# Expert attention on one core: q summed on GpSimd, and three moves in the order of a step

## What is computed

```python
ss, sd = sigmoid(x @ Ws), sigmoid(x @ Wd)          # b t H E
ms, md = topk_mask(ss, 3), topk_mask(sd, 3)
ss_g, sd_g = ss * ms, sd * md
q5 = (x @ Wq).reshape(b, t, H, E, DH)
kv = (x @ Wkv).reshape(b, t, 2, H, E, DH)
k5, v5 = kv[:, :, 0], kv[:, :, 1]
q = einsum('bthed,bthe->bhtd', q5, sd_g)            # k, v alike with ss_g
attn = softmax(einsum('bhid,bhjd->bhij', q * DH ** -0.5, k))
out = einsum('bhij,bhjd->bihd', attn, v)
o5 = einsum('bthd,dm->bthm', out, Wo).reshape(b, t, H, E, 128)
y = einsum('bthem,bthe->btm', o5, md)               # and x = x + y
```

## Time and profile before

| | us |
|---|---|
| median of 3 executions | 2792.57 |
| lowest, highest | 2789.05, 2792.84 |
| the profiled execution, its own time | 2794.09 |
| its span (first to last instruction) | 2792.3 |

### The profile page before, as it was taken

How to read it: one execution, slowest core, us unless ns; L and a number is a source line. 1 busy time by engine, 2 the same in 40 slices (tenths; PEclk the granted TensorE clock), 3 DMA queues, 4 the chain that set the end, 5 groups by cost and what they waited for, 6 DMA issues and landing times. The chain is left out here.

```text
span 2792.3 us, 55544 instructions
## 1 busy us (share of the span) xinstructions
PE 2415.4 (87%) x21310; PEld 1550.2 (56%) x21310; DVE 2030.8 (73%) x3560; ACT 1517.5 (54%) x2069; POOL 1631.0 (58%) x1348
## 2 busy tenths in 40 slices
PE   6787686896999999999778999998697789999986
PEld 3555544643667667666545655555434456555554
DVE  7998455445777777776688888886386888888862
ACT  4222122322888888888435655556362255666663
POOL 1888100001999999999315677777500156777775
PEclk9999788987999999999899999999898999999998
DMA  1000000002889988999414444445401145444454
GB/s 43 1 1 1 0 23 13 1 22 65 151 152 156 162 153 154 159 159 150 111 30 79 92 92 95 95 95 99 86 1 60 28 77 95 92 92 91 92 103 78
DMA packets 763815, 226.70 MB, mean 81 GB/s; under 512 B 745992, under 2 KB 754696, under 8 KB 763552
## 3 DMA queue, kind: packets, MB, share of 16 engines
q1 hardware_dynamic: 763552, 223.16, 42.9%
HBM read 20.70 MB, written 1.05 MB: 8 GB/s over the span
## 5 line engine op out<-in xcount | busy, mean ns | idle before, releaser
L2274 PE MATMUL banks<-g_w,normed_t 128*128 128x320 f32 x1536 | 506.8, 456 | 72.4 <-DVE g_scratch L2525 69.8
L1575 POOL TENSOR_TENSOR g_p_lo<-g_p,g_p_hi 128x512 bf16<-128x512 f32 (+1 forms) x256 | 418.8, 1656 | 176.3 <-ACT g_p_hi L1559 145.8
L1764 DVE TENSOR_REDUCE at_negmax<-banks 128x1 f32<-128x1024 f32 x256 | 301.6, 1220 | 154.1 <-PE banks L1676 154.1
L2525 DVE TENSOR_TENSOR g_scratch<-banks,g_gate 128x640 f32<-128x640 f32 x384 | 314.2, 821 | 133.0 <-PE banks L2274 131.7
L2274 PEld LDWEIGHTS banks<-g_w,normed_t 128*128 128x128 f32 x1536 | 267.3, 193 | 184.5 <-DVE g_scratch L2525 111.2
L1741 POOL TENSOR_TENSOR at_p_lo<-at_p,at_p_hi 128x640 bf16<-128x640 f32 x256 | 355.4, 1402 | 13.3 <-ACT at_p_hi L1729 11.6
L1552 ACT ACTIVATE g_p<-banks,g_negmax 128x1024 f32<-128x1024 f32 x256 | 286.2, 1118 | 118.7 <-DVE g_negmax L1588 114.5
L2460 POOL TENSOR_TENSOR g_routed<-g_o,g_mask 128x640 f32<-128x640 f32 x128 | 161.1, 1259 | 303.7 <-DVE g_o L1597 303.5
L1588 DVE TENSOR_REDUCE g_negmax<-banks 128x1 f32<-128x1024 f32 x256 | 309.8, 1215 | 27.0 <-PE banks L1499 26.7
L1722 ACT ACTIVATE at_p<-banks,at_negmax 128x1024 f32<-128x1024 f32 x256 | 285.4, 1115 | 6.3 <-DVE at_negmax L1764 6.3
L1499 PE MATMUL banks<-g_k_t,g_q 64*128 64x512 f32 x1024 | 258.0, 623 | 26.7 <-ACT g_k_t L2401 14.0
(11 more groups left out here) (410 smaller groups left out, 5970.6 us busy)
## 6 DMA issues: line engine op xcount, KB each, us to landing
at_swapped<-at_crossed SPq DMA_DIRECT2D x128, 128.0 KB, 2.8
g_w<-in_ex_w SPq DMA_DIRECT2D x2, 2880.0 KB, 11.5
f_w<-in_W SPq DMA_DIRECT2D x2, 1024.0 KB, 5.7
at_rope<-in_rope SPq DMA_DIRECT2D x1, 2048.0 KB, 10.0
at_t_hi<-at_p_hi SPq DMA_TRANSPOSE x128, 3.6
at_t_lo<-at_p_lo SPq DMA_TRANSPOSE x128, 3.6
g_t_hi<-g_p_hi SPq DMA_TRANSPOSE x128, 4.0
g_t_lo<-g_p_lo SPq DMA_TRANSPOSE x128, 3.8
```

What stands on the lines that cost most here:

```text
L1575: self.nc.gpsimd.tensor_tensor(self.part(self.p_lo, j, h), self.p[:, j % 2, h, 0:self.WIDTH[h]], self.part(self.p_hi, j, h), ALU.subtract) ...
L1764: self.nc.vector.tensor_reduce(self.negmax[:, j % 2, h:h + 1], self.core.banks[:, first:first + 2, :], AX.XY, ALU.max, negate=True).then_i ...
L2274: nc.tensor.matmul(out[:, 0:ED], core.xt[:, at:at + P], w[:, kind * H + tile // (T * BATCH) * 2 + h, :], start=True, stop=True).then_inc(p ...
L2525: v.tensor_tensor(qk_product[:, tile % 2, kind] if kind < 2 else v_product[:, tile % 2], core.banks[:, bank:bank + 2, 0:ED].rearrange("p h ...
```

## The change

Four things, in both expert attention stages:

1. q is no longer reduced on DVE. Its weights are laid out expert by expert (`ex_w`), its gate product is stored so, and POOL sums the five experts with three `tensor_tensor` adds: two experts with two, one with one, and the fifth (`sum_queries`). DVE's `sum_tile` becomes `sum_keys`, which reduces k alone. The semaphore `tok_ready` becomes `q_ready` and `k_ready`. POOL does ten tiles before its step loop, and the q sum of tile j + 10 in step j between `pool_lo` and `route(j-1)`.
2. PE: beside(0) goes ahead of transpose(j), and subtract(j) behind values(j-1, 0) and beside(1).
3. DVE: dve_normalise(j-1) goes ahead of beside(2).
4. ACT: act_rest(j) goes behind act_exp(j+1, 1), and act_hi(j+1, 1) behind it and behind the copies of `place`.

```diff
--- before.py
+++ after.py
@@ -2164,7 +2164,8 @@
         beats = [sb(f"beats{e}", [P, 6 * 2 * TILES, E - 1 - e]) for e in range(E - 1)]
         lost = sb("lost", [P, 6 * 2 * TILES, E - 1])
         scratch = sb("scratch", [P, 6 * 2 * ED])
-        qk_product = scratch[:, 0:4 * 2 * ED].rearrange("p (t k h c e) -> p t k h c e", t=2, k=2, h=2, e=E)
+        q_product = scratch[:, 0:2 * 2 * ED].rearrange("p (t h e c) -> p t h e c", t=2, h=2, e=E)
+        k_product = scratch[:, 2 * 2 * ED:4 * 2 * ED].rearrange("p (t h c e) -> p t h c e", t=2, h=2, e=E)
         v_product = scratch[:, 4 * 2 * ED:6 * 2 * ED].rearrange("p (t h c e) -> p t h c e", t=2, h=2, e=E)
         tok = sb("tok", [P, 2, T, 2, D])
         routed = sb("routed", [P, 2, E, D])
@@ -2180,7 +2181,7 @@
         mask_ready, gates_applied = sem("mask_ready"), sem("gates_applied")
         proj_full = sem("proj_full")
         product_ready = sem("product_ready")
-        tok_ready = sem("tok_ready")
+        q_ready, k_ready = sem("q_ready"), sem("k_ready")
         v_ready = sem("v_ready")
         qk_full, qk_ready = sem("qk_full"), sem("qk_ready")
         zt_full, zt_ready = sem("zt_full"), sem("zt_ready")
@@ -2206,13 +2207,13 @@
             i = n - first(j)
             return (j + T, 2, i) if i < 2 else (j + LEAD, (i - 2) // 2, i % 2)
 
-        def last_of(tile, value):
-
-            if value:
+        def last_of(tile, kind):
+
+            if kind == 2:
                 return 4 * T + 2 * tile + 1 if tile < T else first(tile - T) + 1
             if tile < T:
-                return 4 * tile + 3
-            return 6 * T + 4 * (tile - T) + 3 if tile < LEAD else first(tile - LEAD) + 5
+                return 4 * tile + 2 * kind + 1
+            return 6 * T + 4 * (tile - T) + 2 * kind + 1 if tile < LEAD else first(tile - LEAD) + 2 * kind + 3
 
         def row_of(tile):
             return tile // T % BATCH * T + tile % T
@@ -2275,7 +2276,7 @@
                                  start=True, stop=True).then_inc(proj_full, 1)
 
             def turn(unit, m, out):
-                pe.wait_ge(tok_ready, unit * T + 4 * (m // 2 + 1))
+                pe.wait_ge(k_ready if m % 2 else q_ready, unit * T + 4 * (m // 2 + 1))
                 for t in range(4):
                     ins = nc.tensor.transpose(out[:, t * P:(t + 1) * P], tok[:, m % 2, 4 * (m // 2) + t].rearrange("p h c -> p (h c)"),
                                               core.ident[:])
@@ -2338,14 +2339,14 @@
                     hs.scores(pe, j + 1)
                 if unit + 1 == UNITS and t > 2:
                     project_out(*done_in(t - 1)[1])
+                beside(0)
                 hs.transpose(pe, j)
                 for k, tile in finishing[0:1]:
                     turn_out(k, tile)
-                beside(0)
-                hs.subtract(pe, j)
                 if j:
                     hs.values(pe, j - 1, 0)
                 beside(1)
+                hs.subtract(pe, j)
                 for k, tile in finishing[0:1]:
                     project_out(k, tile)
                 if turning:
@@ -2425,17 +2426,18 @@
                     hs.act_exp(act, j + 1, 0)
                 for k, tile in finishing[0:1]:
                     place_out(k)
-                hs.act_rest(act, j)
                 if not last:
                     hs.act_hi(act, j + 1, 0)
                 if t == 0 and unit:
                     hs.act_split_values(act, unit, (v_ready, (unit + 1) * T))
                 if not last:
                     hs.act_exp(act, j + 1, 1)
-                    hs.act_hi(act, j + 1, 1)
+                hs.act_rest(act, j)
                 if t in (2, 6) and unit + 1 < UNITS:
                     for i in range(2):
                         place(unit + 1, t // 4 * 2 + i, core.ps[i])
+                if not last:
+                    hs.act_hi(act, j + 1, 1)
                 for k, tile in finishing[1:2]:
                     place_out(k)
             for t in (T, T + 1):
@@ -2467,10 +2469,23 @@
                     step(g.tensor_tensor(z[:, tile, :], z[:, tile, :], two, ALU.add))
                 pool.sem_inc(z_ready, 1)
 
+            def sum_queries(tile):
+                unit, t = tile // T, tile % T
+                if t in (0, 4) and unit:
+                    pool.wait_ge(qk_full, unit * 4 - 2 + t // 2)
+                pool.wait_ge(product_ready, (last_of(tile, 0) + 1) // 2)
+                part = q_product[:, tile % 2]
+                step(g.tensor_tensor(part[:, :, 0:2], part[:, :, 0:2], part[:, :, 2:4], ALU.add))
+                step(g.tensor_tensor(part[:, :, 0], part[:, :, 0], part[:, :, 1], ALU.add))
+                g.tensor_tensor(tok[:, 0, t], part[:, :, 0], part[:, :, 4], ALU.add).then_inc(q_ready, 1)
+
+            for tile in range(LEAD - 1):
+                sum_queries(tile)
             for j in range(STEPS):
-                unit, t = j // T, j % T
                 for h in range(2):
                     hs.pool_lo(pool, j, h)
+                if j + LEAD - 1 < TOTAL:
+                    sum_queries(j + LEAD - 1)
                 if j:
                     route(j - 1)
             route(STEPS - 1)
@@ -2520,26 +2535,29 @@
                 tile, kind, _ = kind_of(n)
                 dve.wait_ge(proj_full, n + 2)
                 if tile >= 2:
-                    dve.wait_ge(tok_ready if kind < 2 else v_ready, tile - 1)
+                    dve.wait_ge((q_ready, k_ready, v_ready)[kind], tile - 1)
                 row = 2 * row_of(tile)
-                v.tensor_tensor(qk_product[:, tile % 2, kind] if kind < 2 else v_product[:, tile % 2],
-                                core.banks[:, bank:bank + 2, 0:ED].rearrange("p h (c e) -> p h c e", e=E),
-                                gate[:, tile // (T * BATCH), 1 if kind == 0 else 0, row:row + 2, :].unsqueeze(2).to_broadcast([P, 2, D, E]),
-                                ALU.mult).then_inc(product_ready, 1)
+                own = gate[:, tile // (T * BATCH), 1 if kind == 0 else 0, row:row + 2, :]
+                src = core.banks[:, bank:bank + 2, 0:ED]
+                if kind == 0:
+                    v.tensor_tensor(q_product[:, tile % 2], src.rearrange("p h (e c) -> p h e c", e=E),
+                                    own.unsqueeze(3).to_broadcast([P, 2, E, D]), ALU.mult).then_inc(product_ready, 1)
+                else:
+                    v.tensor_tensor((k_product if kind == 1 else v_product)[:, tile % 2], src.rearrange("p h (c e) -> p h c e", e=E),
+                                    own.unsqueeze(2).to_broadcast([P, 2, D, E]), ALU.mult).then_inc(product_ready, 1)
 
             def sum_values(tile):
                 if tile % T == 0 and tile:
                     dve.wait_ge(hs.v_split, tile // T)
-                dve.wait_ge(product_ready, (last_of(tile, True) + 1) // 2)
+                dve.wait_ge(product_ready, (last_of(tile, 2) + 1) // 2)
                 v.tensor_reduce(hs.v[:, tile % T, :, 0:D], v_product[:, tile % 2], AX.X, ALU.add).then_inc(v_ready, 1)
 
-            def sum_tile(tile):
+            def sum_keys(tile):
                 unit, t = tile // T, tile % T
                 if t in (0, 4) and unit:
                     dve.wait_ge(qk_full, unit * 4 - 2 + t // 2)
-                dve.wait_ge(product_ready, (last_of(tile, False) + 1) // 2)
-                v.tensor_reduce(tok[:, :, t].rearrange("p k h c -> p k (h c)"),
-                                qk_product[:, tile % 2].rearrange("p k h c e -> p k (h c) e"), AX.X, ALU.add).then_inc(tok_ready, 1)
+                dve.wait_ge(product_ready, (last_of(tile, 1) + 1) // 2)
+                v.tensor_reduce(tok[:, 1, t], k_product[:, tile % 2], AX.X, ALU.add).then_inc(k_ready, 1)
 
             def add_out(k, tile):
                 dve.wait_ge(y_full, k + 1)
@@ -2560,9 +2578,9 @@
             for tile in range(T):
                 apply_gates(4 * tile, 0)
                 if tile:
-                    sum_tile(tile - 1)
+                    sum_keys(tile - 1)
                 apply_gates(4 * tile + 2, 2)
-            sum_tile(T - 1)
+            sum_keys(T - 1)
             dve.wait_ge(gates_ready, CHUNKS)
             choose((0,), range(T, 2 * T), range(E - 1))
             keep((0,), range(T, 2 * T))
@@ -2578,11 +2596,11 @@
                 n = 6 * T + 4 * (tile - T)
                 apply_gates(n, 4)
                 if tile > T:
-                    sum_tile(tile - 1)
+                    sum_keys(tile - 1)
                 else:
                     hs.dve_split_values(dve, 0)
                 apply_gates(n + 2, 6)
-            sum_tile(LEAD - 1)
+            sum_keys(LEAD - 1)
             for j in range(STEPS):
                 unit, t = j // T, j % T
 
@@ -2605,11 +2623,11 @@
                     hs.dve_split_values(dve, unit)
                 if j + T < TOTAL:
                     sum_values(j + T)
-                beside(2)
                 if j:
                     hs.dve_normalise(dve, j - 1)
+                beside(2)
```

(4 more changed lines are left out.)

## The result

The changed kernel takes 2770.7 us (median of 5 executions, 2768.09 to 2782.5), the kernel before 2792.57 (5 executions, 2789.05 to 2793.61). That is 21.9 us less. In all that follows, medians and ratios leave out two executions that ran far outside the rest, one of tail_act_old (3977.98 us, mean granted clock 0.553) and one of half_tail (4722.54 us, clock 1.000). The forecast was 2747, 45.6 faster; 2770.7 lies in the range, but less than half of the forecast gain came. The profiled execution took 2769.47, its span is 2767.7, and the mean granted clock 0.942.

A forecast was written before the change was run, and what follows sets the result against it. PE and DVE, holding each other through one pair of projection banks, were taken as the bound. The terms summed to 23.0 us a stage, 46 for two, off 2794.1: 2748, given as 2747 against the median; range 2727 to 2777.

The forecast's parts named there:

- prologue: Eight tiles before the steps: bank hand-over binds instead of DVE, tiles 2.3 apart instead of 2.86; 5.2 us a stage.
- steps 0 to 4: Steps in which DVE chooses experts: PE waits for DVE, so DVE's whole 1.06 a step counts; 5.3 us a stage.
- units 2 to 5: Within steps 17 to 53, with q sum and three-part routing: GpSimd sets the pace, 8.40 against 8.60, 0.20 a step.
- The last ten steps: End of each stage, no q sums: ACT's second exponential comes 0.5 earlier; 1.5 us gained, between 0 and 3.
- Four q sums beside the choosing: Early steps: 0.5 lost at each, in POOL's slack, so nothing; if DVE were held, up to 4 us on both stages.
- 0.42 of extras: Turning of q and k and split of v add 0.42 to the mean step; PE and DVE would need 8.2.
- plain step: Steady step of PE and DVE: bank hand-overs sum to 7.77, taken as 7.8, against 8.18 before.
- POOL's step: Steps with three-part routing: 6.57 without waiting plus 1.78 for three q adds, 8.35 us.
- Rival A: Steps 17 to 53: GpSimd's adds make it slower once POOL's step passes 9.02; 2813 us, chance 0.09.
- Rival B: Steady steps gain nothing, from slower POOL adds or an unchanged bank chain; 11.7 a stage, 2769 us, chance 0.18.
- C: POOL is quicker: adds at 1.64, step 8.2; 32.9 us a stage, 2727 us, chance 0.14.
- D: Whole kernel: waits only change place and POOL eats the rest; within 0.2% of before, chance 0.05.

The follow-up runs named there:

- tail_act_old: Changed kernel with ACT's order of before in unit 7 alone, PE's new; 2768.82 us, ratio 0.9919.
- half_tail: Changed kernel with every second q tile from tile 24 on summed by DVE, and PE's and ACT's old orders in unit 7; 2753.39 us.
- tail_old: Changed kernel with PE's and ACT's orders of before in unit 7 alone; 2759.94 us, ratio 0.9880.
- tail_pe_old: Changed kernel with PE's order of before in unit 7 alone, ACT's new; 2762.26 us, ratio 0.9901.
- q_only: Changed kernel with q summed on GpSimd but the orders of PE, DVE and ACT as before; 2767.23 us, ratio 0.9905.
- orders_only: Kernel before with only the new orders of PE, DVE and ACT, q still summed with k on DVE; 2793.42 us, ratio 1.0003.
- pool_less: Changed kernel without the second of POOL's three q adds, so two experts are missing from q; 2740.3 us, ratio 0.9814.
- pool_more: Changed kernel with the second of POOL's three q adds made twice; 2807.67 us, ratio 1.0059.
- quarter_tail: Changed kernel with every fourth q tile from 25 on summed by DVE, and PE's and ACT's old orders in unit 7; 2751.38 us.
- half_dve: Changed kernel with every second q tile from tile 24 on summed by DVE, new orders kept in unit 7; 2756.97 us, ratio 0.9873.

## Why the prediction fell short

By its own terms, a stage:

| term | forecast | measured, first / second stage |
|---|---|---|
| prologue, steps 0 to 4, and the steps up to the end of unit 1 | about 14 | 14.9 / 13.1 |
| units 2 to 5 | 32 x 0.20 = 6.4 | 5.0 / 5.4 |
| units 6 and 7 | 5 x 0.20 + 1.5 = 2.5 | -6.8 / -7.3 |
| sum | 23.0 | 13.1 / 11.2 |

Forecast 14 is 5.2 + 5.3 + 3.6. The second stage's first row is the 24.31 gained at its last g_o less the first stage's 13.06, with the other rows taken off; what little lies between the stages is in it. These are the two profiled executions, 24.6 us apart.

**The step that failed** is "*The last ten steps* have no q sums; ACT's second exponential comes 0.5 earlier, which the scores wait for in some: **1.5**, between 0 and 3." It weighed waits alone and took PE's durations from rows at a granted 1.00. Those steps lose about 7 us a stage, outside both bounds. I had moved PE's subtraction behind the values without asking what stands between them when the projections have run out; tail_old shows that the new orders of PE and ACT in unit 7 cost 10.8 of the roughly 14 us, and tail_pe_old that PE's alone costs 8.4; it is the granted clock that costs it, since a step of either order at 1.00 takes 8.89. Nearly all the rest is in unit 6 of the second stage, where steps of 10.91 and 10.36 stand at a clock of 0.84. Neither half of the change alone does that: q_only has 62.25 there, orders_only 62.08. What in the two together does it is open. The step of 10.91 holds a wait of 2.02 for a transpose that took 5.54, and it is absent in pool_less, with a faster POOL; a second one, of 10.29 at 0.83, is there too (unit 63.24). No run takes the new orders out of unit 6 alone.

**Too small** was the price of POOL's collisions. Four q sums beside the choosing were put at nothing, "in slack of POOL", with "4 us on both" if DVE were held: DVE was held. The choosing grew from 12.7 to 16.5 a stage, 7.6 us on both. It fits with unit 0, which gained 3.9 and 1.6 where steps 0 to 4 and the steps behind them were to give over 5; a larger gain before the first g_o, 7.95, made up for it. That the first row of the table is near its 14 is luck in part. The tiles of the prologue are 2.40 apart in the mean (starts of L2560 from 1385.62 to 1400.01 are six) against 2.86 and a forecast of 2.3. The split of v was counted in the 0.42 of extras at its old price and not against POOL's pace: 0.7 to 1.0 a unit over the 66.6 of POOL alone, where the forecast of 8.40 a step left 0.6. The difference makes the units 0.3 to 0.4 longer than forecast, which is the 1.0 to 1.4 a stage missing from units 2 to 5.

**Right** were the parts from single rows: 7.77 for a plain step of unit 1 and of all steps in which POOL has slack; POOL's step, 8.33 where 8.35 was forecast (the adds take 0.73, 0.46 and 0.46 where 0.64, 0.52 and 0.52 were put, so that two errors of size cancel, which is luck); 0.81 for the reduce of k, measured as 0.82; POOL's wait for g_o gone (no such wait from unit 3 into unit 6 of the second stage, where before it was 1.55 to 3.17 us a step). The g_o starts in units 2 to 5 were to be 8.3 to 8.5 apart; that is their mean alone, for they go by 7.77 and 8.1 and then 9.5 to 11. The forecast called 1.78 us for 0.66 in agreement with the Trainium skill (GPSIMD Engine Reference, Engine selection), which has GpSimd about twice as slow; it is 2.7 times. Rival A has the right mechanism and never reached its turning point of 9.02 (its 2.73 for three adds at 0.86 is 2.68 by its own terms). pool_more, with POOL's step at 8.86, loses all the same: 10.9 and 12.4 us a stage in units 2 to 5, and 9.4 and 10.5 in units 6 and 7, where the forecast had a gain. Rival B's 2769 is nearest in time and for another reason: the steady steps do gain. C's faster POOL was tried in pool_less, by leaving out an add. D, the order does nothing, was named with 0.05: as a whole the orders are worth nothing measurable to this kernel, 2767.23 without them against 2770.7 with them, but each piece moves time. In unit 7 alone they lose 11, in unit 0 of orders_only they lose 9 and 12, and in steady units they gain 2.6 where POOL leaves them the room.

## What to carry to other kernels

Cost an order of instructions in every regime that it runs through: the tail, where the filler work has ended, had the same code and the opposite sign (11 us lost in unit 7, 2.6 a steady unit gained), and an order for the steady state can be switched off there with one condition. Work moved to an engine with slack brings that engine's collisions too; list which two-input instructions of the other will now lie beside it, and check each for both sides. When the receiving engine ends within a few tenths of the bound, move a part of the tiles, not all (here three quarters, quarter_tail).

## What the runs showed of the hardware

- The granted clock of TensorE stood at 0.82 to 0.83 in steps in which PE was busy 82 to 85% of the time, with no wait longer than 1.36 us; the same program did so in one stage and not in the other (half_dve). A step then costs 10.5 to 10.7 instead of 8.89.
- A DMA transpose of g_t_lo takes 3.8 us from issue to landing, but 13 of the changed kernel's 15 beside which a packet of the queue "q8 instruction" started took 4.7 to 5.7, and PE waited up to 2.0 us for them.
- A DVE reduce of 640 elements into 128 takes 1.27 with the summed elements 64 apart and 0.81 side by side.
- Collisions of DVE and POOL lengthened both: a split of 1.24 to 2.50, a POOL add of 0.73 to 1.74.
- Open: whether those packets are what holds up the transposes; and what in PE's new order brings the clock down in one stage and not in the other.
